# Moving the split activations of a mixture-of-experts kernel to other SBUF offsets modulo 512 bytes

## The reference

```
xn = layernorm(x)
s  = C(scan(B(xn)))          # h_t = A * h_{t-1} + (xn B_w^T + B_b); y = h C_w^T + C_b, 256 states
logits = xn Wr + br          # 8 experts, the best 2 of each token, softmax over the two
g  = silu(sum over the two experts of c_e * ((silu(xn W1_e) * (xn W3_e)) W2_e))
out = x + s * g
```

## Time and profile before

| | us |
|---|---|
| median of 3 runs | 781.85 |
| lowest, highest | 780.06, 781.9 |
| the profiled execution | 784.27 |
| its span, first to last instruction | 782.5 |

### The profile page before, as it was taken

How to read it: one execution, slowest core, us unless ns; L and a number is a source line. 1 busy time by engine, 2 the same in 40 slices (tenths; PEclk the granted TensorE clock), 3 DMA queues, 4 the chain that set the end, 5 groups by cost and what they waited for, 6 DMA issues and landing times.

```text
span 782.5 us, 17098 instructions
## 1 busy us (share of the span) xinstructions
PE 752.0 (96%) x5366; PEld 674.0 (86%) x5366; DVE 521.8 (67%) x1079; ACT 374.5 (48%) x664; POOL 506.2 (65%) x507
## 2 busy tenths in 40 slices
PE   4999989999999999999999999999999999999895
PEld 2554449999999999999999999999999999999784
DVE  6988975676777667666866665556556664544776
ACT  3985243555455445444544553445455654442440
POOL 4742837788477866856783687476648746564595
PEclk9999999999999999999999999999999999999998
DMA  9999913534565545435544644263537554953996
GB/s 288 338 316 323 152 30 120 136 64 74 129 144 112 101 89 115 65 53 139 138 69 101 168 62 82 42 141 68 108 76 195 101 128 87 313 108 40 278 368 223
DMA packets 101983, 111.16 MB, mean 142 GB/s; under 512 B 15648, under 2 KB 89376, under 8 KB 101888
## 3 DMA queue, kind: packets, MB, share of 16 engines
q0 software_dynamic: 25920, 35.54, 27.5%
q1 hardware_dynamic: 50032, 50.34, 20.3%
q10 hardware_dynamic: 25936, 24.33, 10.4%
HBM read 66.74 MB, written 43.45 MB: 141 GB/s over the span
## 4 chain that ended last, share of the span: by engine, by line
PE 71%; DVE 9%; DMA 7%; issue 6%; POOL 3%; ACT 2%; ACTq 1%; DVEq 0%; POOLq 0%; SPq 0%
PE bank L1555 13%; PE bank L1556 13%; PE bank L1557 12%; PE bank L1581 12%; PE bank L1582 6%; DMA y_rows<-y_sb,token_at 5%; PE bank L1455 4%; PE bank L1689 4%; DVE xnT L1105 2%; PE bank L1543 2%; POOL y_rows L622 2%; DVE stats L976 1%; PE bank L1418 1%; PE bank L1607 1%; PE bank L1608 1%
## 5 line engine op out<-in xcount | busy, mean ns | idle before, releaser
L622 POOL DMA_INDIRECT y_rows<-y_sb,token_at x128 | 216.3, 1690 | 135.5 <-DVE y_sb L1223 60.9
L1555 PE MATMUL bank<-parts,W_sb 128*128 128x256 f32 x1008 | 283.1, 281 | 0.3
L1556 PE MATMUL bank<-parts,W_sb 128*128 128x256 f32 x1008 | 282.2, 280 | 0.0
L1557 PE MATMUL bank<-parts,W_sb 128*128 128x256 f32 x1008 | 281.1, 279 | 0.0
L1555 PEld LDWEIGHTS bank<-parts,W_sb 128*128 128x128 f32 x1008 | 189.7, 188 | 2.6 <-DVE parts L1171 0.8
L1556 PEld LDWEIGHTS bank<-parts,W_sb 128*128 128x128 f32 x1008 | 189.5, 188 | 0.0
L1557 PEld LDWEIGHTS bank<-parts,W_sb 128*128 128x128 f32 x1008 | 189.2, 188 | 0.0
L1581 PE MATMUL bank<-W_sb,parts 128*128 128x512 f32 x512 | 184.5, 401 | 1.1 <-DVE y_sb L1223 1.0
L1211 DVE TENSOR_TENSOR hbuf<-hbuf,bank 128x512 f32<-128x512 f32 x128 | 87.2, 686 | 145.7 <-PE bank L1557 129.8
L613 POOL DMA_INDIRECT xg<-xn_rows,token_at x128 | 144.3, 1127 | 38.1 <-issue 19.2
L1582 PE MATMUL bank<-W_sb,parts 128*128 128x256 f32 x512 | 142.7, 279 | 0.0
(11 more groups left out here) (253 smaller groups left out, 939.5 us busy)
## 6 DMA issues: line engine op xcount, KB each, us to landing
x_late<-L_attn_x SPq DMA_DIRECT2D x24, 512.0 KB, 10.0
raw<-L_ffn_W ACTq DMA_DIRECT2D x24, 512.0 KB
odd_raw<-L_ffn_W ACTq DMA_DIRECT2D x21, 512.0 KB
xn_rows<-h_sb SPq DMA_DIRECT2D x16, 512.0 KB, 6.5
y_rows<-xnT SPq DMA_DIRECT2D x4, 2048.0 KB, 15.7
yy<-y_rows SPq DMA_DIRECT2D x16, 512.0 KB, 9.1
out<-x_late SPq DMA_DIRECT2D x11, 512.0 KB, 7.4
x_kept<-L_attn_x SPq DMA_DIRECT2D x4, 512.0 KB, 6.6
```

Of the source, the lines that this page charges most:

```text
L622: return eng.indirect_dma_start(out=y_rows, out_offset=rows, in_=y, in_offset=None, bounds_check=T + TW - 1, oob_is_err=True, compute_op=A ...
L1555: eng.matmul(part, high, x_h, start=k == 0, stop=False)
L1556: eng.matmul(part, low, x_h, start=False, stop=False)
L1557: last = eng.matmul(part, high, x_l, start=False, stop=k == KD - 1)
```

## The change

No instruction is added, removed or moved: on each engine the order and the shapes of all instructions are the same before and after. Only the places of operands in SBUF change. In bytes per partition, modulo 512 and counted from the weights:

| operand | before | after |
|---|---|---|
| x, high and low, block k = 0 | 192 | 384 |
| x, high and low, block k = 1 | 320 | 448 |
| h high, buffer 0 and 1 | 384, 448 | 448, 448 |
| h low, buffer 0 and 1 | 448, 0 | 0, 0 |
| first pair tile's x, all blocks | 0 | 384 |
| odd tile's x high and h high | 0, 0 | 448, 448 |
| odd tile's x low and h low | 0, 0 | 0, 0 |

`before_high` and `before_low` are tensors that nobody uses; they only take room.

```
         with ExitStack() as odd:
             odd_raw = sb("odd_raw", [P, W_COLS], f32, odd)
             odd_W = sb("odd_W", [P, 2 * W_COLS], f32r, odd)
+            before_high = sb("before_high", [P, 112], f32, odd)
             odd_xh = sb("odd_xh", [P, KD * P], f32r, odd)
+            odd_hh = sb("odd_hh", [P, I], f32r, odd)
+            before_low = sb("before_low", [P, 16], f32, odd)
             odd_xl = sb("odd_xl", [P, KD * P], f32r, odd)
+            odd_hl = sb("odd_hl", [P, I], f32r, odd)
             odd_h = sb("odd_h", [P, I], f32, odd)
-            odd_hh = sb("odd_hh", [P, I], f32r, odd)
-            odd_hl = sb("odd_hl", [P, I], f32r, odd)
...
-        X_STEP, H_STEP = 288, 1040
+        X_STEP, H_STEP = 272, KI * TW
...
-        xh, xl = x_part(32), x_part(672)
-        hh, hl = h_part(1232), h_part(3296)
-        first_xh, first_xl = (odd_W[:, n * KD * TW:(n + 1) * KD * TW].rearrange("p (k n) -> p k n", k=KD) for n in range(2))
+        xh, xl = x_part(80), x_part(720)
+        hh, hl = h_part(1248), h_part(3312)
+        first_xh, first_xl = (odd_W[:, 96 + n * KD * TW:96 + (n + 1) * KD * TW].rearrange("p (k n) -> p k n", k=KD) for n in range(2))
```

More of the change, by code:

```diff
@@ L164, in build @@
             plan_work = sb("plan_work", [P, 2 * KD * P + 3 * I], f32, planning)
-        del pad_to_weights, odd_weights
+        del pad_to_weights, odd_weights, before_high, before_low
         def x_of(c):
```

## The result

The changed kernel takes 782.25 us (median of 20 runs, 780.74 to 784.9) against 781.41 us of the kernel before (20 runs beside it): ratio 1.0016, 95% interval 1.0009 to 1.0024. It is slower by some 1 us, where 773 was forecast.

What follows compares the result with a forecast made beforehand. TensorE's matmul start intervals were taken as the bound. Gains of 1.3 (h), 0.35 and 0.75 (odd tile), 0.2 (first tile) and 6.4 (x) summed to 9.0 us, giving 773 us; range 767 to 786.

Steps and rivals of the forecast that it cites:

- What bounds the kernel, and one nanosecond per matmul arrives: Expert stage: TensorE, busy 96% of the span, bounds it; time is matmul count times the interval between starts.
- The duration as a ladder of intervals in steps of 1 ns: TensorE's matmul rows: shown duration moves with the start interval, some 162 to 164 ns above it.
- h, buffer 0 to 2.82 us, 1.3 us less: Down projection: buffer 0 gets buffer 1's offsets, its blocks fall from 2.86 to 2.82 us, 1.3 us in sum.
- The odd tile, 1.1 us less, first tile 0.2: Odd tile's h gains 0.35 us and its x 0.75 us; the first pair tile's x gains 0.2 us.
- x, 6.4 us less: Gate and up of the other 63 tiles, 3024 matmuls: only distance counts, mean interval 0.115, 2.1 ns less each.
- the side counts: Rival for x in gate and up: 118 to 119.5 ns, 2.7 to 7.3 us more; total 782 to 786.5, chance 0.25.
- The two independent read ports: Rule against the forecast: moving operand and weight load read SBUF independently, no offset matters, x would gain nothing.
- Another engine takes over: Rival: an engine other than TensorE becomes the bound; 25% spare seen in the tiles, not priced, no chance given.

Runs made afterwards that it cites:

- x_0: The changed kernel with both blocks of x, and the first pair tile's x, at 0: 789.12 us, ratio 1.0097 to the kernel before.
- x_448: The changed kernel with both blocks of x, and the first pair tile's x, at 448: 779.27 us, ratio 0.9968 to the kernel before.
- the repeated matmul: Whole computation left out, TensorE alone repeating one matmul 40 times per operand distance: settled means 120.0, 117.8, 120.0, 113.3 ns at 0, 64, 128, 192.
- the bare one: Whole computation left out, TensorE alone running the kernel's own matmul sequences over operand places: gate and up 116.7 ns at (192, 320), 118.2 at (384, 448).

## Why the prediction was wrong, step by step

- *What bounds the kernel, and one nanosecond per matmul arrives:* right. x_0 shows 7.8 us more in the gates and ups and 7.6 at the end.
- *The duration as a ladder of intervals in steps of 1 ns:* right to about 2 ns only. An interval of 117.8 is shown as 281 ns in the slow tiles of x_448 and as 279 in the repeated matmul at 64.
- *h, buffer 0 to 2.82 us, 1.3 us less:* right in the trace for the block (2.86 to 2.81; on average 31 ns, 1.0 us). Not foreseen: buffer 1, with unchanged offsets, lost 0.6 of it again, since more of its blocks settled on 350 ns a pair.
- *The odd tile, 1.1 us less, first tile 0.2:* right in sign, 0.3 and under 0.1 in size.
- *x, 6.4 us less:* this is the step that failed, "I take it that only the distance counts and not which stream is ahead". It went 2.2 us the other way. Three of its parts fell: the distance repeats after 256 bytes, so that 384 and 448 are 128 and 192, and the old 192 and 320 were 192 and 64; 64 on one side is 117.8 ns and on the other 113.3; and there is no interval "of an offset" at all to be added up, since two blocks that alternate have an interval of their own (118.2, not the mean 116.7 of theirs). For the same reason the 0.113 and 0.1165 that were carried over from the down projection couldn't be carried to x: there h's 448, loaded, is on the side on which the repeated matmul has 117.8, and yet the pair ran at 0.113 a matmul. Nor is a third of a pair an interval of 256 columns: repeated alone, the matmul of 512 columns is shortest at distance 0 (226.7 ns) and longest at 192 (233.3), where that of 256 columns is longest at 0 and shortest at 192. The rows had a hint against it: distance 0 had the longest interval in the earlier trace rows, yet the low part of the faster buffer stood at distance 0 as well.
- *The rival "the side counts", 782 to 786.5:* the measured time, 782.25, lies in it, and that a side exists is shown. But the number agrees by luck: its mechanism, a line from 117.1 to 119.5 as the distance nears 512, is not what the runs show: at 448 with both blocks x is at its best.
- *The two independent read ports* (the Trainium skill, SBUF — State Buffer, "Who interferes with whom"): the runs with TensorE alone show intervals of 113.3 to 120.0 ns for the same matmul by the place of its operands, so some coupling is there. The rule's other half agrees with the runs: the gates and ups of the busy full kernel settle on the intervals of the bare one, so no other engine added to them here. No block of 256 columns came under 113.3 ns; the floor of 109.2 was not reached.
- *Another engine takes over:* not at the size of this change; at 5.9 us less, with h at (448, 384), TensorE waited 1.4 us for h's low part, which VectorE makes.

Still open: what in the chip makes the period of 256 bytes and the modes. The runs show that the place of both operands and what runs in front decide, not by which part; that it is the moment of entry is the reading that fits all of them. Why the full kernel's block grew by less than the bare one is open as well. The odd tile's own places weren't searched.

## What to carry to other kernels

Where matmuls of four-byte float32r, the only type tried here, follow one another without a gap, read the distance between their starts, not their durations, and compare blocks of the same line: differences of 1 to 6% at equal shapes come from where the operands lie and how the block is entered. Such a setting can't be judged from one pair of operands, nor added up over edits: time the real sequence with its neighbours, TensorE alone, over all places in one kernel, then try the best few in the full one. A local optimum in one block (h at 448 and 0) can push the next block into its slow mode.

## What the runs showed of the hardware that wasn't expected

- One matmul of 256 float32r columns with a load of 128 x 128 in front of each: 113.3 to 120.0 ns between starts, by (streamed minus loaded offset) modulo 256 bytes; 512 columns: 226.7 at distance 0 to 233.3 at 192 (eight distances in steps of 64), the other way round from 256 columns.
- Two modes at the same addresses, 113.3 and 117.8 ns, chosen at the entry (240 or 248 columns in the matmul in front) and kept for 48 matmuls (in one tile, until a wait). The down projection has two as well, 340 and 350 ns a pair.
- With both operands moved together by 64 to 448 bytes, the interval stayed at 120.0 in all eight blocks, and with only the loaded one moved by 64 or 192 it was 113.3 or 117.8, as by the difference: the relative place counts. Only 128 apart it was 118.7 with the loaded operand ahead and 120.0 with the streamed one.
- The settled intervals of gate and up in the bare kernel and in the full one, with ScalarE, VectorE, GpSimd and DMAs at work, agree within 0.5 ns.
